# A GNN and mixture-of-experts kernel: the low part of one weight chunk in sixteen is made by GpSimd

## The reference, cut to what matters

```python
h2 = _ln(x, ln2_g, ln2_b).reshape(-1, d)
gate_logits = h2 @ Wg                                    # 8 experts
w, sel = jax.lax.top_k(gate_logits, 1)
hid = relu(einsum('nd,edf->enf', h2, W1) + b1)           # W1: (8, 768, 3072) f32
y = einsum('enf,efd->end', hid, W2) + b2                 # W2: (8, 3072, 768) f32
moe = einsum('ne,end->nd', combine, y)
```

## Time and profile before

| | |
|---|---|
| time before, median of 3 runs | 928.65 us (924.72 to 932.22) |
| time of the profiled execution | 930.92 us |
| its span, first to last instruction | 929.4 us |
| mean granted TensorE clock in it | 0.971 of full speed |
| busy: PE | 874.0 us, 94% |
| busy: DVE | 705.7 us, 76% |
| busy: ACT | 556.4 us, 60% |
| busy: POOL | 90.3 us, 10% |
| tiles 1 to 7 | about 517 to 914 us of the span |

### The profile page before, as it was taken

The page is one execution under the profiler, slowest core; times in us unless marked ns, Lnnn a source line. Parts: engine busy times, 40 slices in busy tenths (PEclk is TensorE's granted clock), DMA queues, the critical chain, the costliest instruction groups (busy, mean ns, idle before and its releaser), DMA issues.

```text
span 929.4 us, 14804 instructions
## 1 busy us (share of the span) xinstructions
PE 874.0 (94%) x5460; PEld 842.0 (91%) x5460; DVE 705.7 (76%) x1060; ACT 556.4 (60%) x780; POOL 90.3 (10%) x88
## 2 busy tenths in 40 slices
PE   7999898989998888899889999999999999999998
PEld 7899897989998667689889989999999999999996
DVE  7997155784333899855559889898998989898895
ACT  5503223154323788842548778787887878787870
POOL 2000006031000400012050000000000000000041
PEclk9999788999999999999799999999999999999998
DMA  7020006348114910060189999999999999999984
GB/s 228 3 101 1 1 2 119 85 101 183 55 51 112 326 71 2 1 185 1 36 254 327 331 349 354 376 335 377 363 361 377 354 378 344 379 358 368 369 288 130
DMA packets 116008, 196.01 MB, mean 211 GB/s; under 512 B 33828, under 2 KB 83196, under 8 KB 115958
## 3 DMA queue, kind: packets, MB, share of 16 engines
q1 hardware_dynamic: 107796, 169.08, 54.7%
q0 software_dynamic: 6336, 24.19, 7.8%
q10 hardware_dynamic: 1826, 2.06, 0.8%
HBM read 177.40 MB, written 17.90 MB: 210 GB/s over the span
## 4 chain that ended last, share of the span: by engine, by line
PE 43%; DVE 29%; DMA 13%; issue 7%; ACT 7%; SPq 0%; DVEq 0%; ACTq 0%
DVE wlo L894 14%; PE ps L1323 13%; DMA raw<-in_L_ffn_W 12%; PE ps L1499 7%; PE ps L1675 5%; PE ps L1694 5%; ACT whi L599 3%; DVE pr L1094 2%; DVE hTT L892 2%; DVE pTl L894 2%; PE ps L1352 1%; PE ps L1559 1%; DVE pr L1101 1%; DVE ohs L945 1%; DMA xs<-in_x 1%
## 5 line engine op out<-in xcount | busy, mean ns | idle before, releaser
L894 DVE TENSOR_TENSOR wlo<-raw,whi 128x2304 fp32r<-128x2304 f32 x137 | 350.9, 2570 | 23.7 <-ACT whi L599 23.5
L599 ACT ACTIVATE whi<-raw 128x2304 fp32r<-128x2304 f32 x139 | 296.2, 2132 | 83.4 <-DMA raw<-in_L_ffn_W 34.3
L1694 PE MATMUL ps<-whi,hTT 128*128 128x384 f32 x768 | 201.6, 339 | 1.0 <-ACT oh7T L599 1.0
L1694 PEld LDWEIGHTS ps<-whi,hTT 128*128 128x128 f32 x768 | 139.2, 188 | 1.2 <-ACT oh7T L599 1.2
L1675 PE MATMUL ps<-whi,hgh 128*128 128x384 f32 x384 | 134.1, 349 | 2.8 <-DVE hgl L894 2.8
L1675 PE MATMUL ps<-whi,hgl 128*128 128x384 f32 x384 | 130.3, 339 | 0.0
L1675 PE MATMUL ps<-wlo,hgh 128*128 128x384 f32 x384 | 129.8, 338 | 0.0
L1694 PE MATMUL ps<-wlo,hTT 128*128 128x384 f32 x384 | 129.0, 336 | 0.0
L1675 PEld LDWEIGHTS ps<-whi,hgh 128*128 128x128 f32 x384 | 73.3, 191 | 2.9 <-DVE hgl L894 2.9
L1675 PEld LDWEIGHTS ps<-wlo,hgh 128*128 128x128 f32 x384 | 73.2, 191 | 0.0
L1675 PEld LDWEIGHTS ps<-whi,hgl 128*128 128x128 f32 x384 | 73.0, 190 | 0.0
(11 more groups left out here) (282 smaller groups left out, 1761.6 us busy)
## 6 DMA issues: line engine op xcount, KB each, us to landing
raw<-in_L_ffn_W SPq DMA_DIRECT2D x128, 1152.0 KB, 6.9
hs_d<-bc POOLq DMA_DIRECT2D x13, 384.0 KB, 6.3
raw<-in_L_gnn_W SPq DMA_DIRECT2D x4, 1152.0 KB, 6.4
hs<-hs_d POOLq DMA_DIRECT2D x8, 384.0 KB, 5.6
ys_d<-ysb POOLq DMA_DIRECT2D x7, 384.0 KB, 6.0
raw<-in_L_ffn_Wv SPq DMA_DIRECT2D x6, 384.0 KB, 5.8
raw<-in_L_ffn_Wq SPq DMA_DIRECT2D x6, 384.0 KB, 5.2
raw<-in_L_ffn_Wk SPq DMA_DIRECT2D x6, 384.0 KB, 6.0
```

Of the source, the lines that this page charges most:

```text
L599: act.activation(out_, in_, func).then_inc(s, 1)
L894: dve.tensor_tensor(out_, in_, hi_, ALU.subtract).then_inc(s, 1)
L1694: ins = mm(ps[0:CAP, 4 + half, 0:HB], l, rr, start=k == 0 and j == 0 and jj == 0, stop=k == FCH - 1 and j == JW - 1 and jj == 2)
```

## The change

In tiles 1 to 7 the low part of chunk 5, the sixth of W1, is made by POOL and no longer by DVE. POOL does it behind `y_out(t)`, once the high part of chunk 5 is there and the low part of chunk 4 has been counted. Because `s_mlo` has to stay in order, DVE waits ahead of the low part of chunk 6 until POOL has counted chunk 5. Tile 0 stays as it is, apart from a wait of DVE on its own earlier count. SP, PE and ACT have the same instructions as before.

```diff
+POOL_CHUNK = 5
@@ gpsimd
+            def chunk_lo(t):
+
+                n = POOL_CHUNK
+                g.wait_ge(s_mhi, SCH * t + n + 1)
+                g.wait_ge(s_mlo, SCH * t + n)
+                gp.tensor_tensor(wlo[n % SLOTS][:, :], raw[n % RAWS][:, :], whi[n % SLOTS][:, :], ALU.subtract
+                                 ).then_inc(s_mlo, 1)
+
             with g.Fori(1, E) as t:
                 next_in(t)
                 y_out(t)
+                chunk_lo(t)
@@ (the same line in the loop for more than 128 tokens, which is not run)
@@ vector
             def split_lo(n, t):
                 d.wait_ge(s_mhi, SCH * t + n + 1)
+                if n == POOL_CHUNK + 1:
+                    d.wait_ge(s_mlo, SCH * t + n)
                 lo(wlo[n % SLOTS][:, :], raw[n % RAWS][:, :], whi[n % SLOTS][:, :], s_mlo)
@@
-                    if k + 2 < SCH and not (first and k < 2):
+                    if k + 2 < SCH and not (first and k < 2) and (first or k + 2 != POOL_CHUNK):
                         split_lo(k + 2, t)
```

More of the change, by code:

```diff
@@ L584, in _ @@
                     y_out(s + E)
+                    chunk_lo(s + E)
                 y_out(TILES)
```

## The result

| | before | after |
|---|---|---|
| median | 927.11 us (4 runs, 924.72 to 932.22) | 948.39 us (4 runs, 946.54 to 950.55) |
| ratio, 95% interval | | 1.0223 [1.0172, 1.0274] |
| time and span of the profiled execution | 930.92, 929.4 us | 946.54, 945.0 us |
| mean granted clock | 0.971 | 0.972 |
| busy: PE | 874.0 us | 875.8 us |

The change costs 21.3 us by the medians, 2.2%; 20 was forecast. The timelines of tile 3 show why: first DVE, then POOL, ACT and PE over the same ten microseconds.

A forecast was written before the change was run, and what follows sets the result against it. PE's pace was taken to bound tiles 1 to 7. Stalls 14.4 plus clock 6.6 less 1.0 given back made 20.0 us: 948.7 against the median of 928.65, forecast as 949 us, range 931 to 957.

The forecast's parts named there:

- The chain: Tiles 1 to 7: POOL holds `hTT` low 0, delaying `bia` 1, ACT, `hid` 3 and PE; 0.80 chance.
- A: Rival in step 2: `hTT` low 0 gets in before POOL; 0 to 0.5 us a tile, 929 to 932; chance 0.10.
- B: Rival: POOL's operation and `hTT` low 0 run side by side, no hold; 925 to 929 us; chance 0.05.
- C: Rival: POOL takes 7.3 us or more, PE also waits for chunk 5's low part; at 8.3, 965 or more; chance 0.03.
- about 5.3 us: Sign on DVE: each tile's first `hTT` low part, directly behind POOL's start, takes this in place of 0.56.
- The stall: PE waits for `hid` 3: 2.2 us each in tiles 2 to 7, 1.2 in tile 1, sum 14.4.
- The clock: PE's granted clock drops to 0.50 behind four of the stalls, between none and six; 6.6 us more.
- nearest to the one that lost the clock: Six stalls are gaps of about 2.0 us, nearest to the 1.88 us gap followed by clock 0.50, not 1.59.
- Given back: Behind tile 1, slower PE makes transfers less late; 1.0 us taken off 2.3 us of PE waits.
- over ten us after that: Chunks 9 and 10: transfers start later, some 3 us for chunk 10, but PE wants them over ten us afterwards.
- The tail: Behind `turn_hid(3)` of tile 7 to the end: no term in the sum, put at nothing.
- the bound: Tiles 1 to 7: PE's pace limits, busy 321.3 of 323.8 us; faster work elsewhere could give back 4.2 us.

The follow-up runs named there:

- swap: The changed kernel with `bia` 1 moved ahead of `hTT` low 0 on DVE in tiles 1 to 7; 936.87 us, ratio 1.0137.
- behind: The changed kernel with POOL also waiting until `hTT` low 0 of the tile is counted; 944.74 us, ratio 1.0189.
- pieces: The changed kernel with POOL's subtraction as two instructions of 1152 columns; 937.22 us, ratio 1.0119.
- half: The changed kernel with POOL making 1152 of the 2304 columns and DVE the others at the old place; 932.90 us, ratio 1.0071.
- again: The changed kernel run once more with no edit; 948.18 us, ratio 1.0247.
- last_own: The changed kernel with POOL's work only in tiles 1 to 6, DVE making the low part of chunk 5 in tile 7; 939.27 us, ratio 1.0161.
- late: The changed kernel with one more ACT operation of 384 columns ahead of `hid` 3 in tiles 1 to 7; 952.51 us in one execution.
- swap_catch: The kernel of swap with half of DVE's low part of chunk 9 left out in tiles 1 to 7; 934.27 us, ratio 1.0068.
- before_late: The kernel before, without POOL's work, with SP starting the transfer of chunk 9 one count of `s_mlo` later; 941.08 us, ratio 1.0147.
- swap_gather: The kernel of swap with the gathers asked for three chunks earlier (`Y_BACK_AT` 7 for 10); 943.61 us, ratio 1.0183.

## Why the forecast was right, and where it was not

**The chain held, step by step.** POOL's operation of 128x2304 takes 5.16 us against the 5.3 taken; it starts 0.10 us behind the low part of chunk 4; the `hTT` low part right behind it is held for 4.92 us; the wait goes by `bia` 1, `hTT` high 1, the high part of chunk 7 and `hid` 3 to PE. swap, behind, pieces and half each break that chain at another link, and in each PE's wait for `hid` 3 is gone. Of the rivals, A (`hTT` low 0 first) and B (no hold) never occurred in the change; behind has A's order, and gave 945 where 929 to 932 was forecast for A, since the hold then falls on `hTT` low 1 and puts DVE further behind. It isn't quite A: POOL starts 1.4 us behind the low part of chunk 4, some 0.8 us later than A would have it. C was excluded by the 5.16. One sign was misstated: an `hTT` low part of "about 5.3 us" doesn't fit the forecast's own 870.54 to 875.31, which is 4.8; 4.92 was measured, up to 0.41 us behind POOL's end.

By the Trainium skill, GPSIMD Engine Reference, section 3.1, the estimate was 5.06 us; the measured 5.16 lies between it and my 5.3.

**The stall.** 1.81 us in tile 3 where 2.2 was forecast. The three terms that differ: POOL's operation 5.15 for 5.3, from POOL's end to PE 3.88 for 4.06, and PE wanting `hid` 3 at 7.32 us behind the end of the low part of chunk 4 in place of 7.24. Seven stalls of that size are 12.7 us for 14.4. Tile 1, for which 1.2 us was forecast, had a gap like the others (1.62).

**The clock, 6.6 us, was wrong.** The step that failed is "nearest to the one that lost the clock". The gaps came out at 1.62 to 1.67 us, and none of the 20 in after, again and last_own (1.61 to 1.67) lowered the clock. late, at 2.04 to 2.66 us, lost it six times of seven, 1.6 us each. Of the two gaps in rows 11 the shorter was the better guide: no gap in the tiles up to 1.86 us lost the clock in any run, and from 1.88 us on eight of ten did. An error of 0.4 us in the stall was enough to put the gaps on the other side.

**"Given back", -1.0 us, had the wrong sign.** A tile loses 0.37 us (again) to 0.47 us (the first profile) beyond the stall, some 2.6 to 3.3 us for seven. The premise was that PE's slower pace leaves everything else more time. But DVE is set back by more than PE is. In the second half of a tile, a step of DVE (`bia`, a low part, `hTT` low: 733.14 to 736.54 in tile 4) takes 3.40 us, and one of PE 3.46. A setback on DVE is therefore not made good there. The low part of chunk 11 shows what is left, with the start of `turn_hid(7)` of the same tile, PE first, in before and in swap:

```profile
729.37 0.38 PE L1662 MATMUL ps<-ident,hid 128*128 128x128 f32 x2
```

```profile
730.48 2.55 DVE L894 TENSOR_TENSOR wlo<-raw,whi 128x2304 fp32r<-128x2304 f32 x1
```

```profile
725.38 0.38 PE L1678 MATMUL ps<-ident,hid 128*128 128x128 f32 x2
```

```profile
727.68 2.54 DVE L905 TENSOR_TENSOR wlo<-raw,whi 128x2304 fp32r<-128x2304 f32 x1
```

The lag is 1.11 us before, 2.30 here in swap, 1.65 in the change (734.89 to 736.54). Slots for the next tile's weights come free that much later, ACT waits longer for their transfers, and the new tile starts late. swap_catch, which gives DVE 1.2 us back with POOL's operation and its hold untouched, is the run that shows the backlog as a cause of tile time. It doesn't show how large a cause: 0.64 of 1.10 us a tile from tile 3 on, 0.33 of 1.09 over all. The lag doesn't fix the price alone either, for half has a lag of 1.6 and loses 0.17 us a tile, and swap_catch has 1.1 to 1.25 and loses 0.46. The backlog also suggests why swap got only half: during the 1.8 us stall of PE in the change DVE catches up with it, and without the stall the lag is 2.3 in place of 1.6. late, whose stalls are longer, has a lag of 1.1 and a first gather of 3.1 us, as before, which agrees; its lower clock, though, gives DVE time as well. If so, taking one cause away enlarges the other and doesn't give its price back. No run tests this by itself. The forecast's sentence that PE wants chunks 9 and 10 "over ten us after that" looked at the wrong end: nothing is late for these two, but for the first chunks of the next tile.

**The tail, put at nothing, was +3.4 us** in the profiled pair. The step that is missing is the consumer furthest away, POOL's gathers. POOL's first gather is issued beside DVE's low parts of the last chunks. With DVE further behind, more of those are back to back, and the issue lasts longer: 3.1 us beside a block of 2 (before), 6.1 beside 3 (after, half), 9.3 beside 4 (swap, pieces). In each case it ends 1.12 to 1.13 us behind the end of a low part: that of the first in before (897.55 and 898.67), of the second in the change (912.81 and 913.94), of the third in swap (902.81 and 903.94). before_late doesn't fit the count, 5.6 us beside a block of 2, but it too ends 1.13 us behind a low part, its second. Why the issue gets through behind the first in one kernel and only behind the third in another, no run shows. In the change the fifth gather is longer too, 3.45 us in place of 1.20. The gathers land late, DVE's last additions of them come late, the last low part of `y` stands behind these, and PE waits 3.0 to 3.7 us in all kernels with a first gather of 5.6 us or more, and, in the profiled execution of the change, its clock falls there. last_own, swap_catch and late have a gather near 3.1 us and a tail of 53.3 to 53.9; the kernels with one of 5.6 us and more have 55.7 to 59.4, and no PE wait of this kind is in the first three. Of the 3.4 us a part that isn't separated is the clock, which differs from one execution to the next in the tail.

**The sum.** 14.4 + 6.6 - 1.0 + 0 was forecast, 20.0. The traces give about 12.7 for the stalls, nothing for the clock in the tiles, about +3 for the rest of a tile's loss and +3.4 to +5.8 for the tail, 19 to 22. (The profiled pair differs by only 15.6 us, since the execution of before lost some 3.5 us in tile 1.) The mechanism of the stall was right and its term 1.7 us too high. That the time came as close as 948.39 us measured to 948.7 forecast is luck: a clock term of 6.6 us didn't occur, and a term with the wrong sign and one put at nothing came to about the same size.

No form with POOL beat the kernel before; of those that do all of the work half came nearest, at 1.0071. That is as the bound said: PE was busy 321.3 of 323.8 us, and DVE's work could only get in its way. Still open: what swap_catch keeps losing, 6.6 us by the medians; and what in the issue of a gather is kept out by DVE's low parts.

## What to carry to other kernels

Before work moves to GpSimd, look for every VectorE operation with two SBUF inputs that can be issued beside it, and then at what stands behind that operation on VectorE: here the held one needed 0.56 us and nobody waited for it, but the bias behind it was on TensorE's path. An engine whose step is as long as that of the engine that bounds the kernel (here 3.40 and 3.46 us) can't make good a setback, so a hold on it is carried to the end of the tile and can reach the next. When one of two causes that may overlap is removed, expect less than its price; and a clock term near its edge should be carried as a range on both sides, not as a number.

## What the runs showed of the hardware that I had not expected

- The exclusion between GpSimd and VectorE goes by whole instruction in both directions. A 0.56 us operation was held for 4.92 us, seven times of seven; with POOL's work in two instructions it was let in between them (2.43 us), and POOL's second instruction took 3.01 us in place of 2.67.
- The issue of an indirect DMA on GpSimd takes longer beside VectorE subtractions that stand back to back: 3.1, 6.1 and 9.3 us beside two, three and four of them of 2.5 us (with one exception, 5.6 us beside two). The first gather of every run but swap_gather ended 1.12 to 1.13 us behind the end of one of them. The Trainium skill, SBUF — State Buffer, section "Who interferes with whom", infers that such a `tensor_tensor` doesn't hinder the generation of descriptors, and says that it hinders GpSimd's reads. The gather here reads its list of slots from SBUF; no run tells whether the reading of that list or the descriptors are what waits. The measured durations decide: it does wait.
- A gap of PE of 1.61 to 1.67 us left the granted clock at 1.00 in 20 of 20 cases; of the seven of 2.04 to 2.66 us in late, six came with a fall to 0.50, and one of 2.09 us didn't. Length alone doesn't decide: 1.88 us lost it in before, 1.86 kept and 1.95 lost it in swap_gather, 2.06 kept it in before_late.
- A POOL subtraction of 128x2304 takes 5.16 us and one of 128x1152 2.67 us, about twice what DVE needs (2.55 and 1.34).
